# Pre-adding the GELU blocks on GpSimd, and fewer, later sums on TensorE, in a fused attention and feed-forward kernel

## The reference

```python
h = jnp.einsum('btd,hd->bth', x, absmean(W_fc))      # 256 -> 1024, weights -1, 0, 1
h = jax.nn.gelu(h, approximate=False)
h = layernorm(h, ln_w, ln_b)                          # over the 1024 inner features
return jnp.einsum('bth,dh->btd', h, absmean(W_proj))  # 1024 -> 256
```

## Time and profile before

| | us |
|---|---|
| median of three runs | 1990.69 |
| lowest and highest | 1987.35, 1992.80 |
| the profiled execution, time | 1986.25 |
| the profiled execution, span of the trace | 1984.5 |
| busy PE, DVE, ACT, POOL over the span | 1863.5, 1703.3, 1613.8, 558.1 |
| matmuls of `down_projection` (L669, `gh` and `gl`) | 113.7 + 113.5 |
| `gl` on VectorE (L533) | 92.1 |

### The profile page before, as it was taken

How to read it: one execution, slowest core, us unless ns; L and a number is a source line. 1 busy time by engine, 2 the same in 40 slices (tenths; PEclk the granted TensorE clock), 3 DMA queues, 4 the chain that set the end, 5 groups by cost and what they waited for, 6 DMA issues and landing times.

```text
span 1984.5 us, 42329 instructions
## 1 busy us (share of the span) xinstructions
PE 1863.5 (94%) x13873; PEld 697.3 (35%) x13873; DVE 1703.3 (86%) x4778; ACT 1613.8 (81%) x2110; POOL 558.1 (28%) x712
## 2 busy tenths in 40 slices
PE   6799999999689999999999999999999999999986
PEld 6455556555322222222232222223222222222223
DVE  5699999999888988989898898989899898989941
ACT  2466666676169999999999999999999999999992
POOL 0112211221413424142342414234241423424111
PEclk7899999999669999999999999999999999999998
DMA  4133332336531403032241414224141431414012
GB/s 170 36 92 100 100 90 85 94 100 137 98 68 28 66 19 65 18 61 45 53 69 37 71 33 83 45 53 69 37 74 30 83 53 45 69 37 77 18 40 76
DMA packets 161366, 130.36 MB, mean 66 GB/s; under 512 B 95360, under 2 KB 145792, under 8 KB 160808
## 3 DMA queue, kind: packets, MB, share of 16 engines
q1 hardware_dynamic: 161192, 128.21, 29.8%
HBM read 75.79 MB, written 42.99 MB: 60 GB/s over the span
## 4 chain that ended last, share of the span: by engine, by line
PE 45%; ACT 16%; issue 3%; DVE 3%; DMA 3%; SPq 2%; POOL 1%; ACTq 0%; DVEq 0%; POOLq 0%
PE pv L1378 19%; ACT prob L1201 13%; PE st L1365 11%; PE sm L1344 9%; ACT excess L1194 3%; PE sm L1324 3%; PE st L1353 3%; DMA scratch_i<-inverse 1%; DVE pm L1277 1%; DVE sm L1273 1%; DMA Yc<-Y 1%; PE sm L1340 1%; SPq L870 1%; DVE sm L1262 0%; DMA out<-Rt 0%
## 5 line engine op out<-in xcount | busy, mean ns | idle before, releaser
L1201 ACT ACTIVATE prob<-st 128x1024 f32<-128x1024 f32 (+3 forms) x1280 | 1078.7, 900 | 71.4 <-PE st L1365 59.1
L1378 PE MATMUL pv<-prob,V 128*32 128x512 f32 (+3 forms) x5120 | 593.9, 541 | 0.2
L1262 DVE CUSTOM_DVE_ANT_0 sm<-sm,mask 128x128 f32<-128x128 f32 (+3 forms) x1024 | 492.2, 511 | 64.2 <-PE sm L1344 51.9
L1344 PE MATMUL sm<-K,Q 48*128 48x512 f16 (+3 forms) x2112 | 524.7, 349 | 15.8 <-DVE pm L1277 4.3
L1365 PE MATMUL st<-Q,K 50*128 50x512 f16 (+3 forms) x2560 | 485.3, 353 | 28.2 <-ACT prob L1201 19.9
L1158 POOL TENSOR_SCALAR_AFFINE_SELECT prob<-prob 128x256 f32<-128x256 f32 x512 | 206.2, 409 | 944.1 <-ACT prob L1201 938.7
L1277 DVE TENSOR_REDUCE pm<-sm 128x1 f32<-128x512 f32 x640 | 416.9, 684 | 23.7 <-PE sm L1344 22.1
L1273 DVE CUSTOM_DVE_ANT_0 sm<-sm,excess 128x512 f32<-128x512 f32 x448 | 311.3, 716 | 33.0 <-PE sm L1344 25.9
L1344 PEld LDWEIGHTS sm<-K,Q 48*128 48x128 f16 x2112 | 167.5, 94 | 326.0 <-DVE pm L1277 159.0
L1365 PEld LDWEIGHTS st<-Q,K 50*128 50x128 f16 x2560 | 126.9, 93 | 427.7 <-ACT prob L1201 307.7
L1194 ACT ACTIVATE excess<-st 128x1024 f32<-128x1024 f32 x219 | 225.0, 1027 | 17.8 <-PE st L1353 11.1
(11 more groups left out here) (156 smaller groups left out, 1954.6 us busy)
## 6 DMA issues: line engine op xcount, KB each, us to landing
Q<-scratch_q SPq DMA_DIRECT2D x102, 128.0 KB, 4.4
K<-scratch_k SPq DMA_DIRECT2D x102, 128.0 KB, 7.3
x<-in_x SPq DMA_DIRECT2D x18, 512.0 KB, 4.4
scratch_v<-Vs SPq DMA_DIRECT2D x64, 128.0 KB, 2.0
scratch_r<-R SPq DMA_DIRECT2D x16, 512.0 KB, 3.2
V_raw<-scratch_v SPq DMA_DIRECT2D x16, 512.0 KB, 10.0
Rt<-scratch_r SPq DMA_DIRECT2D x16, 512.0 KB, 3.9
Yc<-Y SPq DMA_DIRECT2D x128, 64.0 KB
```

The source lines that it names most:

```text
L1201: act.activation(prob[(slot * UNITS + k) % PT][:, :, 0:width], st[number % ST][:, :, 0:width], ACT.Exp)\
L1262: dve.tensor_tensor_reduce(x, x, mask[:, CH - width:], 1.0, -3e38, ALU.add, ALU.max, pm[:, row, t, k:k + 1]).then_inc(sm_read, 1)
L1344: pe.matmul(dst[:, 0:block_width(t, k)], lhsT=Q[slot][r, h // 2, t * P:(t + 1) * P], rhs=K[slot][r, h // 2, k * CH:k * CH + block_width(t, ...
L1378: i = pe.matmul(pv[2 * DH * h:2 * DH * (h + 1), CH - width:CH], lhsT=V[quad % VSLOTS][:, j, h, :], rhs=prob[(slot * UNITS + 2 * n + h // 2 ...
```

## The change

A new tile `gs` (4 blocks of values and squares, float32) is written by GpSimd: for each j of 0 to 3, block j of `g` plus block j + 4, values and squares in one instruction of 128 x 1024. The four additions stand between GpSimd's `rstd` and its `xc`, and each waits for the square of block j + 4. The sums on TensorE then take the four blocks of `gs`, values and squares, in 8 products in place of 16. They are moved from ahead of `down_projection` 0 and 1 to behind it.

```diff
+        gs = sb("gs", [P, HC // 2, 2, CH])
+        gs_ready = sem("gs_ready")
@@ gpsimd
                     rsqrt(rstd, ve).then_inc(rstd_ready, 1)
+                    for j in range(HC // 2):
+                        pool.wait_ge(g2_ready, ch * HC + HC // 2 + j + 1)
+                        pool.tensor_tensor(out=gs[:, j, :, :], in0=g[:, j, :, :], in1=g[:, HC // 2 + j, :, :], op=ALU.add)\
+                            .then_inc(gs_ready, 1)
                     pool.wait_ge(R_ready, ch + 1)
                     add_constant(1 - par, i2 * 16 + 16 + 16 * par)
@@ tensor
             def sum_strips(ch):
-                pe.wait_ge(g2_ready, ch * HC + HC)
+                pe.wait_ge(gs_ready, (ch + 1) * (HC // 2))
                 for k in range(2):
-                    for hc in range(HC):
-                        q = hc % 4
+                    for q in range(HC // 2):
                         i = pe.matmul(strip_bank[STRIP * q:STRIP * (q + 1), :], lhsT=...,
-                                      rhs=g[:, hc, k, :], start=hc + 4 * k < 4, stop=hc + 4 * k >= 8, tile_position=(0, STRIP * q))
+                                      rhs=gs[:, q, k, :], start=k == 0, stop=k == 1, tile_position=(0, STRIP * q))
@@ tensor, the loop
-                sum_strips(ch)
                 pe.wait_ge(gl_ready, ch * HC + HC)
                 down_projection(ch, 0)
                 down_projection(ch, 1)
+                sum_strips(ch)
                 pe.wait_ge(v_read, ch * 2 + 2)
                 pe.wait_ge(strips_ready, ch + 1)
                 transposes(ch + 1)
```

## The result

| | before | changed |
|---|---|---|
| median, us | 1991.71 (4 runs, 1987.35 to 1992.80) | 2173.52 (4 runs, 2170.59 to 2175.41) |
| ratio, 95% interval | | 1.0916 (1.0898 to 1.0934) |
| span of the profiled execution | 1984.5 | 2172.0 |
| mean distance of two `frs` | 27.88 | 39.21 |
| clock of TensorE, mean of the span | 0.971 | 0.932 |

The direction was right and the size was not: 2099 us was forecast, with 2150 as the upper end, and the time fell on the first rival (2170).

What follows compares the result with a forecast made beforehand. TensorE was taken to set the 27.88 us chunk period. A delay of 5.4 us plus 1.4 of clock loss, 6.8 a chunk over 16, added 109 us to 1986.25; with 4.4 to the median, 2099 us, range 2055 to 2150.

Steps and rivals of the forecast that it cites:

- the first rival: In the second stage, additions also hold the four `xn`; last `gl` 8.7 us late, 2170 us; chance 0.18.
- TensorE sets the period, VectorE has 2.2 us to spare: Second stage: TensorE busy 27.70 of 27.88 us a chunk, VectorE 25.71, leaving it 2.2 us at most.
- A GpSimd addition and a two-input VectorE instruction exclude each other, taking turns: Second stage: a VectorE instruction with two SBUF inputs and a GpSimd one reading SBUF alternate; additions 2.35 us, 0.4 more when waiting.
- The four `xn` have one SBUF tensor input and run through: During the additions, `xn` keep their 1.38 us; only three `gl` are held, the last 4.3 us later.
- The lost cover: With the sums moved, TensorE idles 6.4 us before the down projections; even without any hold, 2.1 us.
- The clock: After TensorE's gap, matmuls restart at half clock, costing 0 to 2.5 us a chunk; 1.4 taken, 22 us over 16.
- my case: Held `gl` plus clock loss in the second stage: 2099 us, from 2072 to 2116; chance 0.70.
- The saving of 1.78 us: Halving the sums' products cuts TensorE's work by 1.78 us a chunk, at most 28.6 us over 16.
- Attention does not change: Attention, after the second stage, reads finished data from memory; a change beyond a few us would show the prediction wrong.

Runs made afterwards that it cites:

- the version with one pair: The kernel before with GpSimd adding only blocks 0+1, `xc` moved beside the PSUM reads, `xn` on VectorE, 14 products ahead of the projections; ratio 1.0010.
- `xn` on VectorE, dealt out evenly: The kernel before with GpSimd adding blocks 0+1 and 2+3, `xc` moved, 12 products spread 3 per column position, `xn` kept on VectorE; ratio 1.0018.
- experiment 2: The changed kernel with the four `xn` moved from VectorE to ScalarE; 2079.2 us, ratio 1.0445.
- experiment 1: The kernel before plus a one-time stretch running ten VectorE instructions alone and beside a GpSimd addition; 2023.2 us (once).
- Experiment 6: The changed kernel with 40 unread matmuls a chunk filling TensorE's gap before the wait for `gl`; 2141.3 us, ratio 1.0755.
- experiment 4: The kernel before with only the sums, still 16 products, moved behind down projections 0 and 1; 2040.6 us, ratio 1.0265.
- experiment 7: The kernel before with one or two GpSimd additions in other places and `xc` moved; three versions, the first with two pairs and `xn` on ScalarE; ratios 1.0013, 1.0027, 1.0010.
- experiment 8: Two-pair versions of experiment 7 with products dealt evenly over column positions: first `xn` on ScalarE, 1978.6 us, ratio 0.9938; second `xn` on VectorE, 1.0018.

## Why the prediction was wrong

By its own steps:
- *TensorE sets the period, VectorE has 2.2 us to spare*: misread, though the sum made no use of it. The busy time left 2.2 us, but these are no reserve. VectorE's waits in that chunk of the kernel before:

```profile
DVE frw L606 <- POOL frs L475: 1.1, 1, 1.1
DVE R L612 <- DVE frw L606: 0.3, 1, 0.3
```

The rest are gaps of about 0.1 us or less between instructions; in that chunk VectorE never waits for TensorE or ScalarE. So both engines set the period, within 0.1 us of each other. With 1.8 us less of VectorE's busy time alone the period was 27.81 (the version with one pair), with 0.86 us less of TensorE's alone 28.09 (`xn` on VectorE, dealt out evenly), and 26.96 only with both relieved.
- *A GpSimd addition and a two-input VectorE instruction exclude each other, taking turns*: held, in the changed kernel for `nmr`, in experiment 2 for `gl`, in experiment 1 for the isolated case.
- **"The four `xn` have one SBUF tensor input and run through": this step failed.** They are each held for one addition or for `xc`, 9.45 us for the four in place of 1.38. The last `gl` came 8.0 us late, not 4.3. The 3.7 us of difference, over 16 chunks, are 59 of the 75 us by which the forecast missed. I had argued against it by comparing durations: 0.35 us for 256 elements against 0.43 for a cast of 512. Experiment 1 shows what the comparison lacked, the fixed time of the form with per-partition scalars. The rule that speaks of `tensor_scalar` in a mode with both ports (Trainium skill, "SBUF — State Buffer", section "Who interferes with whom") was right here, 0.41 us alone and 2.07 beside an addition; I had given it 0.18 because of that comparison. And the trace of before had left a hint unread. The first `xc` (56.54 to 58.89) lay over a `tensor_scalar` too, and this one took 0.41 us, to just behind the end of `xc`, where it takes 0.17 in the chunk of the earlier trace rows:

```profile
58.50 0.41 DVE L511 TENSOR_SCALAR ve<-mv 128x4 f32<-128x4 f32 x1
...
271.02 0.17 DVE L511 TENSOR_SCALAR ve<-mv 128x4 f32<-128x4 f32 x1
```

- *The first rival, 2170 us, last `gl` 8.7 us late*: its mechanism is what happened, 2173.5 and 8.0. It had the holds shifted by one, with the first `xn` free and the `gl` of block 5 held; in the rows all four `xn` are held and that `gl` is free. That its time is only 4 us off is partly luck: a hold that was 0.7 us too long per chunk made up for a lost cover and a clock that were each 0.4 too small, and for 7.8 us in attention that it did not count.
- *The lost cover*: the mechanism held. The move of 16 products alone costs 3.2 us; my figure for lost cover and exposed copy in the sum was 1.1 beyond the holds, which belongs to the case where the hold is already there. Experiment 6 measures that term at the full clock: from the last `gl` to `fst` 11.67 us against 10.19, so 1.5.
- *The clock*: mechanism right, term mis-sized. 1.4 us was taken, 1.8 measured, in a range of 0 to 2.5. The lower end of my case, 2072, left out the 4.4 us between profile and median; it should have been 2077.
- *The saving of 1.78 us*: real in the records (1.92 us for 16), and on the path, since the sums now stand between the last `gl` and `fst`. This stretch is 13.4 us with 16 products moved (experiment 4) and 11.7 with 8 at the full clock (experiment 6), 1.7 less. It was only small against the holds.
- *Attention does not change*: its instructions do not, but its time moved by 7.8 us, more than the few us that I had named as a sign of being wrong (below).

What remains of the miss is about 6 us in the clock, 6 in the lost cover and 8 in attention. (By the spans of the profiles the miss is 78 us, by the medians 75.)

## What to carry to other kernels

In these runs work on an idle GpSimd was free only where VectorE meanwhile read PSUM (with at most one SBUF input) or did statistics. What read two inputs from SBUF, a cast, and a `tensor_scalar` waited for it; only the odd form that wrote rows with gaps did not. List, for the stretch in which GpSimd reads SBUF, what VectorE executes, and treat a float32 `tensor_scalar` from SBUF to SBUF as held unless it was measured beside a GpSimd instruction; its duration alone does not tell. Idle time that an engine's busy share suggests is not a reserve: read what it waits for in one chunk. Before moving a block of matmuls, ask which wait it covered. And count packed matmuls by the fullest column position, not by their number.

## What the runs showed that I had not expected

- **Packed sums last as long as the fullest position.** 16 and 12 products took 3.5 us alike with four on one position; 12 with three on each took 2.7; 8 with two took 1.9: some 0.8 to 0.9 us for each product more on the fullest position.
- **The start of attention depends on when the clock rises.** Granted clock and busy times, first of the kernel before, then of the changed one:

```profile
515.00:577.00 62.00, 44.43 (x145) 11.60 (x145) 49.83 (x164) 15.49 (x19) 22.92 (x22) 0.51 0.46 95
```

```profile
697.00:768.00 71.00, 55.46 (x197) 14.05 (x198) 55.78 (x178) 23.06 (x26) 21.91 (x21) 0.50 0.38 78
```

After the gap between the stages TensorE stays at 1.2 GHz for 62 us in one profile and 71 in the other, although it is busy for over 70% of both. Between the last `frs` and the end the spans are 1469.0 and 1476.8 us. The profiles of the 13 kernels, which all run the same attention, fall into two groups. In four (before, the probes, the first version of experiment 7, the second of experiment 8) the clock rises 59 to 60 us behind the last `frs`, and 1469.0 to 1471.0 us follow that `frs`. In the other nine it rises 73 to 74 us behind it, and 1473.4 to 1478.5 us follow. The two versions of experiment 8, which differ only in where `xn` runs, fall into different groups, so the 7.8 us need not be of the change's own making. What picks the moment no run shows.
- **Useless matmuls can pay.** 40 more matmuls a chunk, with no reader, made the changed kernel 32 us faster.
